# One pre-activation bank, 16 matmuls ahead of the recurrent loop, and unread matmuls in TensorE's gaps within it

## What is computed

```python
def step(carry, tgt):
    s, c, alpha = carry
    f = conv(alpha, conv_w)
    e = einsum('a,bta->bt', va, tanh(enc_proj + (s @ Wa_s.T)[:, None, :] + einsum('bft,af->bta', f, Wa_f) + ba))
    alpha_new = softmax(where(mask, e, -1e30), axis=1)
    g = einsum('bt,btd->bd', alpha_new, hbatch)
    y = tanh(g @ L_gy_w.T + L_gy_b + s @ L_sy.T) @ L_yy_w.T + L_yy_b
    ig, fg, cg, og = split(tgt @ L_ys.T + s @ L_ss.T + g @ L_gs_w.T + L_gs_b, 4)
    c = sig(fg) * c + sig(ig) * tanh(cg)
    s = sig(og) * tanh(c)
```

## Time and profile before

| | us |
|---|---|
| three runs | 1772.58, 1774.41, 1777.65 |
| span of the profiled execution, the only time it has | 1777.0 |
| TensorE busy in it (matmul) | 1506.0 |
| VectorE busy | 919.2 |
| ScalarE busy | 528.9 |
| GpSimd busy | 387.5 |
| mean granted TensorE clock, share of 2.4 GHz | 0.633 |

### The profile page before, as it was taken

The page is one execution under the profiler, slowest core; times in us unless marked ns, Lnnn a source line. Parts: engine busy times, 40 slices in busy tenths (PEclk is TensorE's granted clock), DMA queues, the critical chain, the costliest instruction groups (busy, mean ns, idle before and its releaser), DMA issues.

```text
span 1777.0 us, 43152 instructions
## 1 busy us (share of the span) xinstructions
PE 1506.0 (85%) x15683; PEld 1022.2 (58%) x15683; DVE 919.2 (52%) x4293; ACT 528.9 (30%) x2023; POOL 387.5 (22%) x1030
## 2 busy tenths in 40 slices
PE   6547999999888888888888888888888888887999
PEld 3334454544666666666666666666666666664443
DVE  4996643331555555555555555555555555553422
ACT  1342231221333333333333333333333333331211
POOL 3344321220000222222222222222222222222211
PEclk7658999999555555555555555555555555555999
DMA  8330000001200000000000000000000000000000
GB/s 326 141 115 11 1 1 0 1 1 52 77 0 0 0 0 0 0 0 0 0 0 0 0 0 0 0 0 0 0 0 0 0 0 0 0 0 1 1 24 25
DMA packets 17363, 34.51 MB, mean 19 GB/s; under 512 B 7476, under 2 KB 8675, under 8 KB 17332
## 3 DMA queue, kind: packets, MB, share of 16 engines
q1 hardware_dynamic: 17332, 34.10, 5.3%
HBM read 32.00 MB, written 2.10 MB: 19 GB/s over the span
## 4 chain that ended last, share of the span: by engine, by line
PE 62%; DVE 25%; issue 6%; ACT 5%; POOL 1%; DVEq 1%; SPq 1%; DMA 0%; POOLq 0%; ACTq 0%
PE bank L1243 18%; PE bank L1073 11%; PE bank L1193 6%; PE bank L1088 6%; PE bank L1221 5%; ACT eh L960 4%; DVE interT L746 4%; PE bank L1199 4%; DVE krep L764 3%; PE bank L1213 3%; DVE rinv L755 3%; DVE rs L743 2%; DVE g L760 2%; PE bank L1231 2%; DVE gat L771 2%
## 5 line engine op out<-in xcount | busy, mean ns | idle before, releaser
L1243 PE MATMUL bank<-krep,uh 128*128 128x128 f32 x1024 | 313.1, 461 | 23.6
L1243 PEld LDWEIGHTS bank<-krep,uh 128*128 128x128 f32 x1024 | 237.4, 320 | 92.4 <-DVE krep L764 92.4
L493 POOL TENSOR_TENSOR sscale<-ex,rinv 128x8 f32 x256 | 51.3, 200 | 667.6 <-DVE rinv L755 667.6
L1221 PE MATMUL bank<-eh,krep 128*128 128x4 f16 x2048 | 95.3, 168 | 92.5 <-ACT eh L960 92.5
L764 DVE TENSOR_TENSOR krep<-inv,ahn 128x128 f32<-128x128 f32 x512 | 162.2, 356 | 0.0
L1073 PE MATMUL bank<-xT,wbig 128*128 128x512 f16 x672 | 157.2, 386 | 3.7 <-DVE xT L591 3.7
L743 DVE TENSOR_TENSOR rs<-bank,rin 128x8 f32<-128x8 f32 x256 | 42.8, 167 | 198.1 <-PE bank L1199 198.1
L1221 PEld LDWEIGHTS bank<-eh,krep 128*128 128x128 f16 x2048 | 74.1, 105 | 114.0 <-ACT eh L960 114.0
L963 ACT ACTIVATE xs<-gat 64x8 f32<-64x8 f32 x256 | 53.4, 208 | 288.7 <-DVE gat L771 288.7
L955 ACT ACTIVATE interT<-bank 128x128 f16<-128x128 f32 x256 | 71.2, 278 | 216.9 <-PE bank L1193 216.9
L1181 PE MATMUL bank<-enc,identb 128*128 128x128 bf16 x771 | 128.4, 303 | 0.0
(11 more groups left out here) (201 smaller groups left out, 3044.5 us busy)
## 6 DMA issues: line engine op xcount, KB each, us to landing
wbig<-d_gate_qT SPq DMA_DIRECT2D x4, 896.0 KB, 10.1
wbig<-d_up_qT SPq DMA_DIRECT2D x4, 896.0 KB, 20.7
wbig<-d_down_qT SPq DMA_DIRECT2D x1, 3584.0 KB, 30.5
d_out<-x_sb SPq DMA_DIRECT2D x8, 256.0 KB, 2.0
sscale<-d_gate_sT SPq DMA_DIRECT2D x2, 896.0 KB, 8.6
interT<-d_gate_sT SPq DMA_DIRECT2D x2, 896.0 KB, 14.9
sscale<-d_up_sT SPq DMA_DIRECT2D x2, 896.0 KB, 4.2
interT<-d_up_sT SPq DMA_DIRECT2D x2, 896.0 KB, 4.3
```

The lines of the kernel that those rows point to most:

```text
L1221: ins = mm(bank[4][:, 4 * gp:4 * gp + 4], hg2[:, j, h, gp * P:(gp + 1) * P], e[:, 4 * h:4 * h + 4], start=(first and gp == 0 and j == 0 an ...
L1243: mm(bank[1 - par][:, 0:P], uh[:, h, :], qv[:, h, :, :], start=False, stop=False, skip_group_check=True)
```

## The change

In the loop both steps use `bank[0]` for the pre-activation. `bank[1]` becomes a target that nobody reads. Ahead of the loop, before TensorE waits for the last of the loop's inputs, 16 matmuls of 512 columns go there. In each step a new helper `keep_busy(n)` puts 384 or 512 columns there at five places, 3968 columns in all.

```diff
@@ ScalarE
-                    nc.scalar.activation(th_hi, bank[par][:, 0:P], ACT.Tanh).then_inc(s["th_s"], 1)
-                    nc.scalar.activation(th, bank[par][:, 0:P], ACT.Tanh).then_inc(s["th_full"], 1)
+                    nc.scalar.activation(th_hi, bank[0][:, 0:P], ACT.Tanh).then_inc(s["th_s"], 1)
+                    nc.scalar.activation(th, bank[0][:, 0:P], ACT.Tanh).then_inc(s["th_full"], 1)
@@ TensorE
             down(2 * IT0, IT0, wd, B, last_gates)
+
+            for _ in range(16):
+                mm(bank[1][:], x_part[0][:, 0, 0:P], x_part[0][:, 0, :], start=True, stop=True)
             pe.wait_ge(s["setup_v"], 1)
...
-            def context_part(par):
+            def context_part():
                 for j in range(3):
-                    mm(bank[par][:, 0:P], identb[:], enc3[:, j, :], start=(j == 0), stop=False, skip_group_check=True)
+                    mm(bank[0][:, 0:P], identb[:], enc3[:, j, :], start=(j == 0), stop=False, skip_group_check=True)
+
+            def keep_busy(n):
+                mm(bank[1][:, 0:n], identb[:], hg2[:, 0].rearrange("p h g -> p (h g)")[:, 0:n], start=True, stop=True)
...
                     last.then_inc(s["sp_done"], 1)          # after L1199
+                    keep_busy(384)
                     pe.wait_ge(s["th_s"], l + 1)            # ahead of L1206
...
                         mm(bank[3][:, 0:8], th_hi, vae2[:, j, :], start=False, stop=False, skip_group_check=True)
+                    keep_busy(512)
                     pe.wait_ge(s["th_lo_ready"], l + 1)     # ahead of L1213
...
+                    keep_busy(512)
+                    keep_busy(512)
                     pe.wait_ge(s["eh_ready"], l + 1)        # ahead of L1221
...
                     masks()
-                    context_part(1 - par)
+                    context_part()
+                    keep_busy(512)
+                    keep_busy(512)
                     for h in range(2):
                         pe.wait_ge(s[f"q{h}_ready"], l + 1)
-                        mm(bank[1 - par][:, 0:P], uh[:, h, :], qv[:, h, :, :], start=False, stop=False, skip_group_check=True)
+                        mm(bank[0][:, 0:P], uh[:, h, :], qv[:, h, :, :], start=False, stop=False, skip_group_check=True)
+                    keep_busy(512)
+                    keep_busy(512)                          # ahead of L1193 of the next step
```

More of the change, by code:

```diff
@@ L1176, in masks @@
                 mm(bank[3][:, 0:8], etl[:], etr[:], start=True, stop=False, skip_group_check=True)
-            def context_part(par):
+            def context_part():
                 for j in range(3):
-                    mm(bank[par][:, 0:P], identb[:], enc3[:, j, :], start=(j == 0), stop=False, skip_group_check=True)
+                    mm(bank[0][:, 0:P], identb[:], enc3[:, j, :], start=(j == 0), stop=False, skip_group_check=True)
+            def keep_busy(n):
+                mm(bank[1][:, 0:n], identb[:], hg2[:, 0].rearrange("p h g -> p (h g)")[:, 0:n], start=True, stop=True)
             masks()
-            context_part(0)
+            context_part()
             with pe.Fori(0, S // 2) as i:
@@ L1192, in _ @@
                         pe.wait_ge(s["sl_ready" if st is sl else "sh_ready"], l + 1)
-                        last = mm(bank[par][:, 0:P], was2[:, j, :], st[:].unsqueeze(2).broadcast_to([J, B, TH]),
+                        last = mm(bank[0][:, 0:P], was2[:, j, :], st[:].unsqueeze(2).broadcast_to([J, B, TH]),
                                   start=False, stop=(st is sl), skip_group_check=True)
```

## The result

The changed kernel takes 1753.81 us, median of four runs (1752.67 to 1761.61); the kernel before, run beside it, 1774.27 (1772.58 to 1777.65). The ratio is 0.9896, interval 0.9873 to 0.9918: faster by about 1%. The forecast was 1752.0, in a range of 1740 to 1772. The profiled execution has a span of 1750.9 us, against 1777.0 before, and a mean granted clock of 0.959.

What follows compares the result with a forecast made beforehand. Bound: the loop's ring of short, mutually waiting operations, with TensorE at 1.2 GHz. Clock −28.2, late fillers +5.1, matmuls ahead of the loop +2.4, L1254 after it −1.7: −22.4 us, to 1752.0; range 1740 to 1772.

Steps and rivals of the forecast that it cites:

- ring: Loop's circle of operations each waiting for the one before; TensorE at L1193, L1213, L1231; clock gain 0.11 us a step.
- E: Gap from L1243's load to L1193's last matmul (old lines), two 512-column fillers; at most 0.06 us late, at least nothing.
- B: Gap between L1211 and L1213 (old lines), one 512-column filler; forecast 0.02 us late, on the ring.
- A: Gap between L1199 and L1206 (old lines), one 384-column filler; forecast 0.06 us late, off the ring.

Runs made afterwards that it cites:

- no_entry: Changed kernel without the 16 matmuls ahead of the loop, fillers kept; 1753.22 us, ratio 0.9862 to the kernel before.
- trim_again: Second measurement of the changed kernel without entry matmuls, with 256 columns in A, 448 in B, 512 and 384 in E; 1752.4 us, ratio 0.9877.
- trim: Changed kernel without entry matmuls, with 256 columns in A, 448 in B, 512 and 384 in E; 1752.51 us, ratio 0.9876.

## What to carry to other kernels

In a chain of short operations over several engines the full clock is worth only the places where TensorE stands in the chain, here 0.1 of 4.5 us a step. Unread matmuls can buy it if each gap holds them at full clock; which gap has no slack is told by the signal that the next ring matmul waits for, and the last gap before it is the one to keep clear. Look at more than one part of the loop: here E's slack was gone after 32 steps, when GpSimd had begun other work and a write on VectorE got slower. Leave a margin in the amount: here three quarters of the columns gave a clock that falls now and then, and half of them cost 7% where none at all cost nothing.

## What the runs showed of the chip beyond that

- At three quarters the clock fell for 6.8 us each time, seven times in one execution, and came back by itself; at half it stayed at 0.5 with TensorE recorded busy 399.86 of 400 us. In no_entry it came up behind a stretch with 3.40 of 3.40 us busy. Whether it rises is thus not to be read from the busy share.
- Short matmuls hardly feel the clock (`el` to `sum_done` 0.274 against 0.263 us), long ones do (512 columns start 0.216 us apart at full clock and 0.427 at the low one, in the first steps of no_entry and trim_again).
- A matmul whose start is recorded 0.010 us later behind its signal ended no later (B in trim).
- Where the rows or columns in use change, TensorE pauses: A's filler starts 0.093 us behind the last matmul of L1206, whose own start 0.025 apart, and L1214 starts 0.267 behind that filler, 0.105 more than the 0.162 that 384 columns take by the 0.216 of 512.
- The second write of L764, 128x128 f32 on VectorE, took 0.280 us with GpSimd idle and 0.43, 0.47 and 1.01 us beside instructions of GpSimd that take 0.41, 0.52 and 1.04.
